# A two-feed-forward block with linear attention: the second feed-forward four iterations behind the first, the attention's statistics directly behind the addition

## The reference

```
x = x + 0.5 * ffn(norm(x))
x = x + attention(norm(x))
x = x + 0.5 * ffn(norm(x))

ffn:   probs = sigmoid(x @ router.T)            # 8 experts, the best 2 kept
       combine = the two best, divided by their sum; 0 for the others
       out = sum over experts e of combine[e] * (relu(x @ W1[e])**2 @ W2[e])
attention: q, k, v = x @ Wqkv (16 heads of 8); rotary embedding on q and k
       qf = elu(q * scale) + 1;  kf = elu(k) + 1
       kv = sum over tokens of kf v;  out = (qf @ kv) / max(qf @ sum(kf), 1e-6) @ Wout
```

## Time and profile before

| | us |
|---|---|
| median of three executions | 799.12 |
| lowest and highest | 795.67, 800.61 |
| the profiled execution, device time | 802.07 |
| its span, first to last instruction | 800.3 |
| POOL busy | 686.3 |
| PE busy | 727.1 |
| mean granted TensorE clock | 0.974 |

### The profile page before, as it was taken

How to read it: one execution, slowest core, us unless ns; L and a number is a source line. 1 busy time by engine, 2 the same in 40 slices (tenths; PEclk the granted TensorE clock), 3 DMA queues, 4 the chain that set the end, 5 groups by cost and what they waited for, 6 DMA issues and landing times.

```text
span 800.3 us, 13031 instructions
## 1 busy us (share of the span) xinstructions
PE 727.1 (91%) x3600; PEld 590.2 (74%) x3600; DVE 581.4 (73%) x1832; ACT 597.6 (75%) x1219; POOL 686.3 (86%) x668
## 2 busy tenths in 40 slices
PE   1788788889999999999999999999999987979977
PEld 1566566667888888888888888888887866767755
DVE  3456688777879798878778786978686768577533
ACT  3577677658888879888888888797878766656755
POOL 3778867869999999999999999999999858666875
PEclk9999999989999999999999999999999989989999
DMA  5553023023323311322333233322223311303230
GB/s 178 185 162 131 19 88 106 1 106 107 106 107 120 106 76 63 128 82 107 119 107 120 107 121 106 120 89 91 69 100 105 120 50 57 120 2 119 119 120 26
DMA packets 31159, 79.36 MB, mean 99 GB/s; under 512 B 3312, under 2 KB 14448, under 8 KB 31088
## 3 DMA queue, kind: packets, MB, share of 16 engines
q1 hardware_dynamic: 30800, 78.47, 28.7%
q10 hardware_dynamic: 288, 0.07, 0.1%
HBM read 73.81 MB, written 4.72 MB: 98 GB/s over the span
## 4 chain that ended last, share of the span: by engine, by line
PE 32%; DVE 28%; POOL 13%; issue 13%; ACT 10%; DMA 3%; DVEq 1%; POOLq 0%; ACTq 0%; SPq 0%
DVE hid L1033 7%; POOL h_lo L866 6%; PE bank L508 4%; PE bank L528 4%; POOL root_f L860 4%; PE bank L529 4%; PE bank L530 4%; PE bank L510 4%; PE bank L509 4%; ACT h_hi L738 2%; DVE pick_f L1011 2%; PE bank L597 2%; DMA g_all_f<-rows_f 2%; PE bank L489 2%; POOL x_lo_at L854 2%
## 5 line engine op out<-in xcount | busy, mean ns | idle before, releaser
L866 POOL TENSOR_TENSOR h_lo<-hid,h_hi 128x512 fp32r<-128x512 f32 x384 | 492.9, 1308 | 77.0 <-ACT h_hi L738 76.4
L1033 DVE SCALAR_TENSOR_TENSOR hid<-bank,g_all_f 128x512 f32<-128x512 f32 x384 | 262.2, 684 | 141.5 <-PE bank L510 101.1
L727 ACT ACTIVATE hid<-hid 128x512 f32<-128x512 f32 x384 | 228.7, 621 | 51.8 <-DVE hid L1033 51.7
L738 ACT ACTIVATE h_hi<-hid 128x512 fp32r<-128x512 f32 x384 | 225.6, 620 | 4.9 <-PE bank L530 0.4
L508 PE MATMUL bank<-x_hi_f,w_hi 128*128 128x512 f32 x384 | 166.4, 433 | 15.2 <-DVE hid L1033 15.1
L528 PE MATMUL bank<-h_hi,w_hi 128*128 128x512 f32 x384 | 157.4, 410 | 10.8 <-POOL h_lo L866 10.8
L510 PE MATMUL bank<-x_hi_f,w_lo 128*128 128x512 f32 x384 | 154.7, 403 | 0.0
L529 PE MATMUL bank<-h_lo,w_hi 128*128 128x512 f32 x384 | 154.3, 402 | 0.0
L530 PE MATMUL bank<-h_hi,w_lo 128*128 128x512 f32 x384 | 153.8, 400 | 0.0
L509 PE MATMUL bank<-x_lo_f,w_hi 128*128 128x512 f32 x384 | 153.7, 400 | 0.0
L508 PEld LDWEIGHTS bank<-x_hi_f,w_hi 128*128 128x128 f32 x384 | 74.1, 193 | 40.4 <-DVE hid L1033 24.5
(11 more groups left out here) (102 smaller groups left out, 1019.1 us busy)
## 6 DMA issues: line engine op xcount, KB each, us to landing
g_all_f<-rows_f SPq DMA_DIRECT2D x128, 512.0 KB, 5.5
x_sb<-in_x SPq DMA_DIRECT2D x16, 256.0 KB, 3.3
out_x<-x_sb SPq DMA_DIRECT2D x16, 256.0 KB, 7.0
g_all_f<-in_w SPq DMA_DIRECT2D x2, 768.0 KB, 6.7
con<-in_const SPq DMA_DIRECT2D x1, 584.0 KB, 6.2
rows_f<-g_row_f SPq DMA_DIRECT2D x32, 16.0 KB, 1.4
g_all_f<-in_wqkv SPq DMA_DIRECT2D x1, 192.0 KB, 6.4
con<-in_const ACTq DMA_DIRECT2D x1, 68.0 KB, 3.1
```

Source lines behind the costliest of these rows:

```text
L727: fn(h, h, ACT.Square).then_inc(s_sq[s], 1)
L738: fn(h_hi[:, c, :], hid[:, c % STAGE, :], ACT.Copy).then_inc(s_hhi[s], 1)
L866: gp.tensor_tensor(h_lo[:, c, :], hid[:, c % STAGE, :], h_hi[:, c, :].bitcast(F32), ALU.subtract).then_inc(s_hlo[s], 1)
L1033: v.scalar_tensor_tensor(hid[:, c % STAGE, :], hp[c % 2][:], 0.0, g_all[s][:, EXPERT[c], :], ALU.max, ALU.mult).then_inc(s_z[s], 1)
```

## The change

`SHIFT` becomes 4, so f2's group follows f1's by four iterations, and `T_LAST` falls by one. The attention of group t moves one iteration forward: statistics directly behind f1's addition (place 3), `inv_std` behind POOL's place 1, `norm`, transposition, `q`, `kv` in the same iteration t, the rest in t+1. Every stream gets its own `xT`, and `evacuate_x` waits for its own stream's low part alone. `norm("f2")` moves ahead of `exp_logits("f1")`, into the place of `norm("at")`, which now stands behind `rows_of_weights("f2")`; the transposed attention input is copied one chunk later. Lone f1 groups have their chunks at places 0, 1, 2, 4, 5, 6, 8, 9, 10, 12, 13, 14 (`4 * c // 3`); lone f2 groups keep every second place. The addition of f1 has one form: `back` at the end of the iteration and `add_moe` behind place 2, alone or not. `aside` is left for f2 alone.

```diff
-SHIFT = 5
+SHIFT = 4
...
-        xT = sb("xT", [P, NTOK])
-        xT = {s: xT for s in STREAMS}
+        xT = {s: sb(f"xT_{s}", [P, NTOK]) for s in STREAMS}
...
+        def place_of(s, t, c):
+
+            if not alone(s, t):
+                return c
+            return 4 * c // 3 if s == "f1" else 2 * c
...
             def iteration(t, par):          # PE
                 transpose("f1", t + 2, t, 0)
                 quarter(t, 0, par)
-                state(t - 2)
+                state(t - 1)
...
-                attend(t - 2)
+                attend(t - 1)
                 quarter(t, 2, par)
-                transpose("at", t - 1, t, 2)
+                transpose("at", t, t, 2)
...
-                if alone("f1", t - 1):
-                    back("f1", t)
...
-                q(t - 1)
+                q(t)
...
-                if not alone("f1", t):
-                    back("f1", t + 1)
+                back("f1", t + 1)
...
-                evacuate_x("f1", t + 2, t, 0)     # ACT
-                squares(t - 1, 7)
-                norm("at", t - 1)
+                evacuate_x("f1", t + 2)
+                squares(t - 1, 21, 24)
+                norm("f2", t + 2 - SHIFT)
                 exp_logits("f1", t + 2)
-                squares(t, 0)
-                norm("f2", t + 2 - SHIFT)
-                squares(t, 1)
+                squares(t, 0, 3)
+                squares(t, 3, 6)
                 rows_of_weights("f2", n2)
                 if not live(t - SHIFT):
                     norm("f1", t + 3)
-                if alone("f1", t - 1):
-                    copy_yT("f1", t, t - 1)
-                evacuate_x("at", t - 1, t, 1)
+                norm("at", t)
                 if not alone("f2", t - 1):
                     copy_yT("f2", n2_last, t)
-                squares(t, 2)
-                squares(t, 3)
-                copy_attnT(t - 2)
-                evacuate_x("f2", t + 2 - SHIFT, t, 2)
+                squares(t, 6, 7)
+                evacuate_x("at", t)
+                squares(t, 7, 9)
+                squares(t, 9, 12)
+                copy_attnT(t - 1)
+                evacuate_x("f2", t + 2 - SHIFT)
...
+                if alone("f1", t):
+                    copy_yT("f1", n1, t)
+                exp_k(t)
...
                 remainders(t, 0, 1)               # POOL
+                inv_std("at", t)
                 inv_std("f1", t + 3)
...
-                remainders(t, 12, 13, 14, 15)
-                inv_std("at", t)
-                remainders(t, 16, 17, 18)
+                remainders(t, 12, 13, 14, 15, 16, 17, 18)
...
-                if not alone("f1", t - 1):         # DVE
-                    add_moe("f1", t)
+                add_moe("f1", t)
                 weighted(t, 3)
+                stats("at", t, 0)
                 stats("f1", t + 3, (par + 1) % 2)
                 weighted(t, 4)
+                mean_variance("at", t)
                 take_sigmoid("f1", n1)
                 mean_variance("f1", t + 3)
...
                 take_sigmoid("f2", n2)
-                stats("at", t, 0)
                 weighted(t, 17)
-                mean_variance("at", t)
```

More of the change, by code:

```diff
@@ L332, in alone @@
             return not live(t + 1 - SHIFT) if s == "f1" else not live(t + 2)
[L334 to L336 removed]
         def aside(s, n):
[L340 removed]
+            return s == "f2" and n >= NG - SHIFT and (NG - SHIFT - n) % 2 == 0
         def y_bank(s, n):
             return yp[other[s] if aside(s, n) else s]
+        def place_of(s, t, c):
+            if not alone(s, t):
+                return c
+            return 4 * c // 3 if s == "f1" else 2 * c
         def chunks(t, place, behind=0):
@@ L352, in chunks @@
                     k = place + PLACES * back - start - behind
-                    step = 2 if alone(s, t - back) else 1
                     n = t - back + 1 - off[s]
-                    if live(n) and k % step == 0 and 0 <= k // step < NC:
-                        out.append((s, n, k // step, back))
+                    if live(n):
+                        out += [(s, n, c, back) for c in range(NC) if place_of(s, t - back, c) == k]
             return out
@@ L515, in down @@
                 if c == 0:
-                    two_banks = n <= SHIFT if s == "f1" else n > NG - SHIFT
-                    if two_banks and n >= 2:
+                    if s == "f2" and n > NG - SHIFT:
                         pe.wait_ge(s_x[s], n - 1)
-                    elif s == "f2" and aside(s, n):
+                    elif aside(s, n):
                         pe.wait_ge(s_x["f1"], NG)
-                    elif not two_banks and n >= 1:
+                    elif due(n):
                         pe.wait_ge(s_x[s], n)
-                    if s == "f2" and n == 0:
-                        pe.wait_ge(s_x["f1"], SHIFT)
                     if first_time(s == "f1", n):
@@ L656, in iteration @@
                 quarter(t, 6, par)
-                kv(t - 1, 0)
-                kv(t - 1, 1)
+                kv(t, 0)
+                kv(t, 1)
                 quarter(t, 7, par)
@@ L690, in evacuate_x @@
                 act.wait_ge(s_t[s], value(n + 1))
[L692 to L695, removed]
+                if due(n):
+                    act.wait_ge(s_lo[s], value(n))
                 fn(xT[s][:], tp[:], ACT.Copy).then_inc(s_xT[s], 1)
@@ L717, in rows_of_weights, with squares @@
                 fn(g_row[s][:], tp[0:EXP * TG, 0:P], ACT.Relu, bias=c_cut[0:EXP * TG, 0:1]).then_inc(s_gr[s], 1)
-            def squares(t, j):
-                todo = [k for place in range(CQ * j, CQ * (j + 1)) for k in chunks(t, place)]
+            def squares(t, a, b):
+                todo = [k for place in range(a, b) for k in chunks(t, place)]
                 for k in range(len(todo) + 1):
@@ L802, in iteration @@
                 exp_logits("f2", t + 2 - SHIFT)
-                squares(t, 4)
-                squares(t, 5)
+                squares(t, 12, 15)
+                squares(t, 15, 18)
                 rows_of_weights("f1", t + 2)
@@ L815, in iteration @@
                     copy_yT("f2", n2_last, t)
[L816 to L819, removed]
+                squares(t, 18, 21)
+                exp_q(t)
+                copy_v(t)
+                if alone("f1", t):
+                    copy_yT("f1", n1, t)
+                exp_k(t)
             minus_one = c_mone
@@ L1144, in iteration @@
                     add_moe("f2", t - 1 - SHIFT)
-                k_features(t - 2)
-                q_features(t - 2)
+                k_features(t - 1)
+                q_features(t - 1)
                 weighted(t, 0)
@@ L1161, in iteration @@
                     split_w1()
-                mask_state(t - 2)
+                mask_state(t - 1)
                 weighted(t, 5)
@@ L1209, in iteration @@
                 choose_two("f2", n2)
-                rope_k(t - 1, 0)
+                rope_k(t, 0)
                 weighted(t, 22)
-                rope_k(t - 1, 1)
+                rope_k(t, 1)
                 weighted(t, 23)
-                rope_k_sum(t - 1)
+                rope_k_sum(t)
             pipeline(dve, iteration)
```

28 lines of the change are left out of this document (14 added, 14 removed).

## The result

| | before | after |
|---|---|---|
| median us, 4 runs each | 798.93 | 816.91 (812.11 to 820.49) |
| profiled execution: time, span | 802.07, 800.3 | 820.49, 818.7 |
| PE, POOL busy | 727.1, 686.3 | 732.5, 683.7 |

The account below looks back on a forecast made before the run. POOL and PE were taken as walls of the full iteration, so the gain had to come from the lone ends: 43.57 - 32.17 - 17.5 - 1.1 + 0 = -7.2 us, median 799.12 to 791.9, range 780 to 804.

Parts of the forecast that it names:

- Part 1: Iteration counts with shift 4: one full iteration more, +43.57 us, and one with attention fewer at the end, -32.17.
- Part 4: The rest: DVE's statistics leave the loop once at the end, -1.1 us; SP's transfers, separate xT and simpler aside free.
- the last 1.1: At the end, DVE's statistics leave the loop for one iteration: -1.1 us.
- C: Full iterations: PE's new waits add 1.9 us in each of 11, +21 in all, giving 812; chance 0.14.
- Part 4's price for the transfers: Spread of the weights takes 1.4 + 5.5 us, beside PE's work in the first lone iteration: nothing, at most +0.8.
- Part 2: Lone f1 iterations: four rebuilt ones take 126.2 us against 143.7 for the five before, -17.5.
- clock term: Lone f1 iterations: PE's slower clock behind pauses adds 0.8 us to each of three, 123.8 becoming 126.2.
- Part 3: Full iterations: POOL's floor of 43.0 us stays, the loop gets about 2 shorter without use; change per iteration taken as 0.
- the two nearly cancel: Full iterations: PE's longer wait at attend against a vanishing wait for DVE's first chunk, -0.1 to +0.3 us, taken as 0.
- A: Lone iterations keep their pace: lone f1 part -23.72 us, sum -13.4, giving 785.7; chance 0.27.
- B: Lone f1 drain is worse: the last three iterations cost 2.5 us more each, giving 799.4; chance 0.18.
- second wait: Full iteration, PE at the attention's transposition: rows ready only 0.2 us ahead, or a norm's length of 1.65 late.

Follow-up runs that it names:

- Experiment 2: Changed kernel with only ACT's order altered, the attention's norm always ahead of f1's: 800.2 us, ratio 1.002 to the kernel before.
- Experiment 4: Kernel before with only the sixteen places for lone f1 groups and the one form of f1's addition: 802.39 us, ratio 1.004.
- Experiment 5: Kernel before with only the attention's statistics and aggregate moved early on DVE, where f1 has a partner: 804.62 us, ratio 1.006.
- experiment 1: Changed kernel with mask_state moved on DVE to directly behind chunk 4, ahead of the attention's aggregate: 816.52 us, ratio 1.020.
- experiments 9 to 11: cw_f from scalar operations on the changed kernel with norm and mask moved; pick_f too; cw_f alone on the kernel before: 857.92, 902.64, 860.65 us.

## Why the prediction was wrong

**Part 1 and the drain of Part 4: right.** -33.2 measured for -33.3; with the full iteration it adds, the mechanism of the shift is as told. That the last 1.1 agrees so well has luck in it: no window shows it, one of the drain is 1.0 longer than its like before (27.03 for 26.07), one 1.2 shorter (21.97 for 23.20). The trace has ten full windows; the eleven in my text were miscounted, and C's sum, written as 812, is 812.9 with eleven and 811 with ten. Part 4's price for the transfers failed, see below.

**Part 2, the lone f1 iterations: the mis-sized term, 13.5 us.** Forecast 24.9, then 28.3, 33.6 and 37.0 with 0.8 of clock on each; measured 28.24, 33.78, 36.87, 40.81. I had seen that PE would stand before the attention's rows, and in the third I counted both norms. What failed:
- *Second*: I took POOL's work as its bound (25.2). The chain through PE was longer: rows after 14.0 us, then 19.8 to the next first chunk, nearly all of it PE, its first part at the lower clock. Experiment 2, which moves only the norm, takes 3.9 off.
- *First*: "DVE's first chunk to POOL's first 2.9" was a price of the old places. With the logits behind the third up, which waits for DVE's first chunk, it is 6.3 (26.36 to 32.69 in the chain after). All behind it is as much later: the weight row is copied at 21.8 us and not at 18.8, and the transfers, which end this iteration, land at 28.2 and not between 24.4 and 25.7. Experiment 4 shows the 28.2 without any other edit.
- *Third*: here the norms were counted, and the transposition came sooner than I had it (14.9 for 16.0). What was too small lies behind it: 22.0 us for 17.6 and the 0.8 of clock. The iteration ends on the weight transfers, 8.8 us behind the weight row, which Part 4 had at 1.4 + 5.5 beside other work and at no cost beyond the first iteration; the first of them alone took 3.44. How much sooner the iteration would have ended with quick transfers, no run shows.
- *Fourth*: the transposition at 14.9 again, and 25.9 behind it. Experiment 2 takes 4.2 off the third and 6.8 off the fourth. With the norm moved, the four sum to 123.8, which is only by chance the sum that the forecast had without its clock term.
- *Transition*: I gave it no price; f1's norm stands in the way there too, 3.0.

The clock term had its sign right: granted 0.87 to 0.94 in these windows against 0.93 to 1.00 before, and ten matmuls at 0.43 in the second. I had put 0.8; the rows show 2.0 for the matmuls and 0.7 for the transposes in that window. Little of it is new, though: the second window before has eight matmuls at that distance too (51.50 to 54.49), and experiment 2 keeps seven (66.02 to 68.58) and is 3.9 us shorter all the same. The Trainium skill, "TensorE: Matmul & The Clock Gate", section "What's actually happening", has the throttled state as the normal one; the rows agree, with matmuls 0.43 us apart behind the pause of 6.1 us and 0.23 apart later.

**Part 3, the full iterations: the step "the two nearly cancel" failed, 9.0 us.** PE's wait at `attend` came (0.6, attend 0.74 later), but the wait for DVE's first chunk did not vanish: it went from 0.3 to 0.4. Shortening the loop by 1.1 us of statistics bought nothing: where they stood, DVE now waits for PE's ups instead (0.36 each ahead of the chunks at 419.49 and 423.76; none there before). Counted from `attend`, DVE's last addition of the iteration does come 0.46 us sooner (23.76 for 24.22), but from there to the next first chunk it is 11.7 us for 11.0: in this stretch `chosen_f` takes 0.53 for 0.19, `cw_f` 0.43 for 0.16 and `ka` 0.86 for 0.69, with only `kf` shorter (0.69 for 0.91). Experiment 5 shows the early statistics by themselves at +0.8, nearly all of it ahead of `attend`; experiment 1 takes 0.6 of the 1.0 back. `pick_f` ahead of the mask grew from 0.21 to 1.32, but costs nothing there: experiment 5 has it at 0.21 and `attend` as late. The 0.2 that are left lie behind `attend` (35.48 us for 35.29 in experiment 5), where DVE makes the end of the chain, and are put down to the grown operations from their durations alone; no run isolates them. For f2's `cw_f` the trace shows what changed beside it: before, it ran inside the attention's `inv_std` on POOL, which the change moved away; after, it runs beside POOL's chunks. What decides which iterations are the long ones (43.96 or 45.9) also stays open.

**The rivals.** *A* was wrong: each lone f1 iteration took longer than its like before, by 3.7 to 6.5 us. *B* named the right windows, and the clock and a late weight transfer both showed; its sum was about half as large as needed (7.5 against 13.5): the three windows it names missed by 10.2, and the first, which it leaves out, by 3.3. *C* named the right place and waiting instruction, at 1.0 us a time instead of 1.9; its second wait, at the transposition, did not come: the rows were there 1.4 us ahead, not 0.2. The signs that I had named for B (the third window over 36) and for C (full windows over 44.2, PE waiting for the mask) both came. My error beyond the sizes was to treat B and C as alternatives. They touch different windows and neither excludes the other; -7.2 with B's 7.5 and half of C's 21 is +11, outside the range that I gave.

## What to carry to other kernels

Where an in-order engine stands before a tile, list all that its producer has queued ahead of that tile: four instructions that nobody was waiting for, placed one slot too early, cost 17 of the 18 us here. Work that is moved ahead of an instruction for which the busiest engine waits costs its whole length there (0.8 us here), and what it leaves free behind is worth nothing if its own engine then waits for the busiest one. Rivals that concern different stretches of the time should be summed and not weighed as alternatives.

## What the hardware showed that I had not expected

Beside POOL's chunks, small DVE operations on SBUF take as long as the chunk lets them, not as long as their size says. Mean of the 32 `pick_f` (64 elements, two inputs), 754 ns before, on the page after:

```profile
L1002 DVE TENSOR_TENSOR pick_f<-chosen_f,root_f 128x64 f32<-128x64 f32 x32 | 33.0, 1033 | 7.2 <-POOL root_f L852 7.2
```

The same instruction took 0.21 or 1.31 us by its place, and `cw_f` from 0.15 to 2.86. After the change 26 of the 32 `cw_f` start while POOL works on 512 columns (a chunk or a low part `x_lo`), and each of them ends 0.02 to 0.03 us behind the end of such an operation; the other six take 0.15 to 0.17. Before, 17 start so, and the other 15 take 0.15 to 0.17 again. POOL's small operations do not hold it up: before the change it ran in 0.16 us inside a `rstd_at` of 1.01.

```profile
422.75 1.01 POOL L845 TENSOR_TENSOR rstd_at<-ve_at,c_mhalf 128x4 f32<-128x4 f32 x1
...
423.51 0.16 DVE L989 TENSOR_TENSOR cw_f<-best_f,rtot_f 128x8 f32<-128x8 f32 x1
```

The longest are over twice POOL's 1.3 us chunk. DVE's chunks, which read a bank of PSUM, stay at 0.63 to 0.69 throughout.

The Trainium skill says in "GPSIMD Engine Reference", section "Specifications", that POOL shares its SBUF interfaces with VectorE, with contention for DVE instructions in a two-port mode or with two SBUF inputs. The Trainium skill says in "SBUF — State Buffer", section "SBUF: two separate sides", that the pair is an exclusive lock for a whole instruction. The traces agree for POOL's chunks, whose ends the operations wait for. They do not for two things: `rstd_at` held nothing up, and a `cw_f` of 2.25 or 2.86 us is more than one instruction's hold. The operations of experiments 9 to 11 have one input beside their scalars. For them the Trainium skill, "VectorE: DVE Perf Modes", section "Mode 2×_2P — use both read ports for one tensor", has a mode for fp32 `tensor_scalar` in which both read ports serve one tensor. That they wait (0.22 us with POOL idle, up to 1.35 beside its chunks) fits; that they ran in this mode, no trace shows.
